# Four pairs of cross-attention and expert layer: the front of each expert layer is moved into the attention loop, the loops over sorted rows are reordered, and the third expert layer is written out without GpSimd

## The reference

```python
x = x + tanh(g_xattn[i]) * xattn_i(layernorm(x), ctx)     # i = 0..3
x = x + tanh(g_ffn[i])   * ffn_i(layernorm(x))

# xattn_0 and 3: 16 heads of 16; 3 with rotary positions and a window mask
# xattn_1: 16 heads of 64, keys and queries scaled to length 1, a null key, layernorm of the output
# xattn_2: 16 heads of 64, a given mask
# ffn_0: logits = xn @ Wr + br; softmax; the two largest of 8 experts, hidden 512, gelu, + 1 shared expert
# ffn_1: the two largest of 8, softmax over the two, hidden 1024, relu
# ffn_2: top1 = argmax(xn @ gateW.T + b)
#        out = relu(xn @ wi.T + wi_b + (xn @ A[top1].T) @ B[top1].T) @ wo.T + wo_b
# ffn_3: the two largest of softmax + bias, silu(x w1) * (x w3) @ w2, + 2 shared units
```

## Time and profile before

| | us |
|---|---|
| median of 3 runs | 2068.6 (2065.77 to 2076.95) |
| the profiled execution | 2049.69 |
| its span (first to last instruction) | 2047.9 |
| busy: PE, DVE, ACT, POOL | 1806.3, 1272.5, 974.8, 530.9 |

### The profile page before, as it was taken

How to read it: one execution, slowest core, us unless ns; L and a number is a source line. 1 busy time by engine, 2 the same in 40 slices (tenths; PEclk the granted TensorE clock), 3 DMA queues, 4 the chain that set the end, 5 groups by cost and what they waited for, 6 DMA issues and landing times. The chain is left out here.

```text
span 2047.9 us, 32584 instructions
## 1 busy us (share of the span) xinstructions
PE 1806.3 (88%) x11864; PEld 1478.7 (72%) x11864; DVE 1272.5 (62%) x2264; ACT 974.8 (48%) x1746; POOL 530.9 (26%) x465
## 2 busy tenths in 40 slices
PE   7979899977999966899999699995899799798896
PEld 4658799933677746899997378874577566588885
DVE  6877487564454545688886576666223588555654
ACT  4642367425776731577674154441233255315760
POOL 2112334263233330222222520004000045203334
PEclk9997799989999985899999799995599899789998
DMA  2004387420000003566772200001000000224753
GB/s 81 1 10 145 124 262 241 140 61 21 27 1 1 1 7 134 193 239 228 229 242 93 88 19 1 1 1 55 9 1 1 25 1 1 84 67 145 235 159 111
DMA packets 97238, 178.46 MB, mean 87 GB/s; under 512 B 24897, under 2 KB 62044, under 8 KB 96012
## 3 DMA queue, kind: packets, MB, share of 16 engines
q1 hardware_dynamic: 85594, 146.13, 21.6%
q0 software_dynamic: 11232, 30.69, 5.2%
q10 hardware_dynamic: 288, 0.00, 0.0%
HBM read 149.51 MB, written 27.26 MB: 86 GB/s over the span
## 5 line engine op out<-in xcount | busy, mean ns | idle before, releaser
L1730 POOL DMA_INDIRECT f_block_rows_home<-normed_x,f_token_of_sb x138 | 168.5, 1221 | 480.2 <-PE psum L1776 329.7
L1756 PE MATMUL psum<-f_block_h_sb,f_w1h_home 128*128 128x256 f32 x736 | 212.5, 289 | 30.2 <-DVE f_block_l_sb L1954 11.9
L1756 PE MATMUL psum<-f_block_l_sb,f_w1h_home 128*128 128x256 f32 x736 | 207.6, 282 | 0.0
L1756 PE MATMUL psum<-f_block_h_sb,f_w1l_home 128*128 128x256 f32 x736 | 207.6, 282 | 0.0
L2329 PE MATMUL psum<-a_xT_home,context_w 128*128 128x256 f32 x704 | 179.6, 400 | 14.3 <-PEq L121 13.1
L1766 PE MATMUL psum<-f_w2h_home,f_hidden_h_home 128*128 128x256 f32 x644 | 187.7, 291 | 1.9 <-DVE f_result_sb L1653 0.9
L1766 PE MATMUL psum<-f_w2h_home,f_hidden_l_home 128*128 128x256 f32 x644 | 181.9, 282 | 0.0
L1766 PE MATMUL psum<-f_w2l_home,f_hidden_h_home 128*128 128x256 f32 x644 | 181.9, 282 | 0.0
L1756 PEld LDWEIGHTS psum<-f_block_h_sb,f_w1h_home 128*128 128x128 f32 x736 | 140.8, 191 | 38.5 <-issue 28.6
L2329 PEld LDWEIGHTS psum<-a_xT_home,context_w 128*128 128x128 f32 x704 | 130.5, 195 | 45.5 <-issue 24.9
L2490 ACT ACTIVATE a_probsT_sb<-psum 77x1024 f32<-77x1024 f32 (+1 forms) x128 | 131.0, 1023 | 65.7 <-PE psum L2381 63.6
(11 more groups left out here) (327 smaller groups left out, 4066.2 us busy)
## 6 DMA issues: line engine op xcount, KB each, us to landing
f_w_sb<-in_f_w SPq DMA_DIRECT2D x161, 512.0 KB, 5.1
sorted_y<-f_result_sb SPq DMA_DIRECT2D x69, 256.0 KB, 2.2
normed_x<-f_xn_all SPq DMA_DIRECT2D x3, 2048.0 KB, 7.5
f_b_row_sb<-in_f_b SPq DMA_DIRECT2D x46, 128.0 KB, 3.5
f_w_sb<-in_f_w SPq DMA_DIRECT2D x23, 256.0 KB, 4.5
f_block_rows_home<-normed_x,f_token_of_sb POOLq DMA_INDIRECT x138, 4.3
residual<-in_x SPq DMA_DIRECT2D x8, 256.0 KB, 6.1
context_w<-in_a_wk SPq DMA_DIRECT2D x2, 1024.0 KB, 5.0
```

What stands on the lines that cost most here:

```text
L1730: nc.gpsimd.indirect_dma_start(block_rows[b % 2][:, h, :], None, xs, bass.IndirectOffsetOnAxis(ap=column, axis=0)).then_inc(sems[f"rows_in ...
L1756: last = nc.tensor.matmul(hid_ps(q)[:, m, :], w, rhs, start=(j == 0), stop=(j == len(parts) - 1))
```

## The change

1. **Front into the attention loop.** A new `front_part` is called inside `attend`. Per batch b, with its output at step s: variance on DVE at s+1 (in a1, where LAG is 3, this and all that follows 3 steps later), power on GpSimd, rows normalised on DVE at s+2, turned on PE at s+3, copied on ACT, multiplied by the router on PE at s+4, logits out on DVE at s+5. Turned rows and logits are two new uses of the spare banks. The loop is 3 steps longer (6 in a1). The rows are stored to `normed_x` batch by batch. The bias row of the shared expert (f0) and of f2 are added by GpSimd there, and the router's, shared expert's and f2's weights are loaded in the attention stage. The tables for sorting are made once in the first stage.
2. **Expert stages** begin with the choice (`Choice`, `find_rows`, `choose_low_rank`).
3. **f2** is written out: ACT rounds weights, inputs and low-rank weights, DVE makes their low parts, GpSimd has no instruction, the gate is a constant, there are no bias products.
4. **Loops over sorted blocks:** PE's order is turn of b+2, first products of b+1, second products of b; ACT takes b+2 (was b+1), DVE splits b+2 (was b+1).
5. **Context part of a1:** ten value products stand ahead of the keys' normalisation, and `take` is apart from `squares`.
6. **Combining in the tail:** f0 combines up to 1, 7, 32 of the 32 pairs behind the three blocks (was 10, 21, 32), f3 4, 12, 20, 32 (was 8, 16, 24, 32).

```diff
+def front_part(env, pair, n):
...
+    def variance(dve, b):
+        for tile in range(b * TPB, (b + 1) * TPB):
+            last = nc.vector.bn_stats(stats[:, tile, :], x[:, tile, :])
...
+        nc.vector.tensor_scalar(var[:, tiles(b)], mv[:, tiles(b), 1], EPS, None, ALU.add).then_inc(sems["var_done"], 1)
+    def power(pool, b):
+        pool.wait_ge(sems["var_done"], b + 1)
+        nc.gpsimd.tensor_tensor(rstd[:, tiles(b)], var[:, tiles(b)], half[:, tiles(b)], ALU.pow)...
+    def add_row(pool, b):
+        pool.wait_ge(sems["normed"], b + 1)
+        nc.gpsimd.tensor_tensor(x[:, tiles(b), :], x[:, tiles(b), :], row[:]..., ALU.add)...
+    def turn(pe, b, bank):
+        pe.wait_ge(sems["normed"], b + 1)
...
+    def route(pe, b, bank):
+        pe.wait_ge(sems["staged"], b + 1)
...
+    def logits_out(dve, b, bank):
+        dve.wait_ge(sems["routed"], b + 1)
...
 # attend
-    FIRST, LAST = -Q_AHEAD, GROUPS + 3
+    LAG = 3 if own else 0
+    FIRST, LAST = -Q_AHEAD, GROUPS + 6 + LAG
+        if rows_at(s) is not None:
+            uses.append(("rows", rows_at(s)))
+        if logits_at(s) is not None:
+            uses.append(("logits", logits_at(s)))
 # attend, tensor, behind output(...)
+                if rows_at(s) is not None:
+                    front["turn"](pe, rows_at(s), take_spare(pe, "rows", rows_at(s)))
+                if logits_at(s) is not None:
+                    front["route"](pe, logits_at(s), take_spare(pe, "logits", logits_at(s)))
 # attend, vector
-                if output_at(s - 1) is not None and not own:
-                    statistics(output_at(s - 1))
+                if output_at(s - 1 - LAG) is not None:
+                    front["variance"](dve, b)
+                if normed_at(s) is not None:
+                    front["normalise"](dve, normed_at(s))
+                if logits_out_at(s) is not None:
+                    front["logits_out"](dve, logits_out_at(s), spare("logits", logits_out_at(s)))
 # routed_experts, tensor
         def body(b, i, s, ahead):
             for u in range(per_expert):
+                if u == per_expert - 1 and ahead >= 2:
+                    turn(b + 2, *later(i, s, 2))
                 if u + 1 < per_expert:
                     first(b, i, s, u + 1)
                 elif ahead:
                     first(b + 1, *later(i, s, 1), 0)
-                if u == per_expert - 1 and ahead >= 2:
-                    turn(b + 2, *later(i, s, 2))
                 second(b, i, s, u)
 # routed_experts, vector
-                if u == 0 and not silu and not begins(b) and ahead >= 1:
-                    split_block(b + 1, (s + 1) % 2)
+                if u == per_expert - 1 and ahead >= 2:
+                    split_block(b + 2, s % 2)
 # context_part, a1, tensor
+        for j in range(VALUES_FIRST):
+            value_products(pe, j)
 # experts (f2), scalar and vector, in place of gpsimd
+        high(w1h[0][:], w1raw[0][:], "w1_high")
+        t["exponentials"](act)
+        high(xh[:, :, chunk(0)], xT[:, :, chunk(0)], "x_high")
...
+        weight_lows(0, 1)
+        x_low(0)
+        low(lbl[:], lb[:], lbh[:], "lora_low")
+        inputs_low(0)
...
```

1055 lines of the change are left out of this document (501 added, 554 removed).

## The result

The changed kernel takes 2054.5 us (median of 14 runs, 2044.9 to 2061.2), the kernel before 2065.5 in the same set (14 runs): a ratio of 0.9938, interval 0.9918 to 0.9959. That is 13 us faster by the ratio and 11 by the medians. In a later set it was 2026.9 against 2045.8 (0.9923, 0.9892 to 0.9953), 16 or 19 us. The forecast was 33 us (0.984): right in sign and inside its range, but almost three times what the first set shows and about twice what the later one does.

The account below looks back on a forecast made before the run. PE was taken as the bound, by its work, lower clock and waits. Terms 58 - 61.5 - 54 + 17.4 + 1.5 + 5.5 + 1 - 1 = -33 took 2068.6 to 2036 us; range 1994 to 2060.

Parts of the forecast that it names:

- Attention loops, +58 forecast: Loops a0 to a3: added turn and router products plus new waits lengthen the four loops by 58 us; lower bound 32.
- a1 (14.2 forecast): a1's loop: query products wait for the turned rows' copy on ACT, about 0.9 us a block; 14.2, bounds 8 and 25.
- rival 3: DVE and GpSimd hold each other up in the attention loops, mattering in a0 and a3: 22 us, 2058; chance 0.10.
- a2, 23.7 forecast: a2's loop: value products wait 2.9 us a block for DVE's late logits read-out; 23.7 us, bounds 8 and 45.
- Rival 4: a1 and a2: late read-outs cost PE a whole softmax step per block, 59 us more, 2095; chance 0.05.
- Fronts removed, -61.5: f0, f1, f3: only a short tail remains before the choice, saving 20.8, 19.7 and 21.0 us.
- f2, -54: a2's last output product to f2's products' end: 159 us against 212.7, first product at 25.8; bounds -60 and -42.
- f0's loop, +17.4: f0's sorted blocks: period rises from 6.73 to 7.6 us over 20 blocks, +17.4; bounds -9 and +30.
- The circle: f0's loop: turn, copies, weight splitting and result read-out run serially between second products, which need the freed bank; 7.6 us.
- Context part of a1, +15.9: Value products wait for read-outs and delay key squares: last key at 516 against 512; +5.5 net, bounds -8 and +10.
- 1 (no wait bites): Attention loops grow by PE's work alone (+32) and f0's loop gains 9: 1984 us; chance 0.20.
- 2: Larger waits: a1 and a3 at upper bounds, f0's loop +30, f2 -42; 2085 all together, two give 2060; chance 0.10.

Follow-up runs that it names:

- second profile: For the changed kernel: the same kernel run again, no edit, 2026.9 us, 0.9923. For the kernel before: run once more, no edit, 2065.7 us, 1.0019.
- the run four: Changed kernel with result read out first in f0 and f1, logits read ahead of softmax in all attention stages, a1's old context order: 1948.8 us, 0.9549.
- Result first: Changed kernel with DVE reading out block b-1's result ahead of the block's and weights' low parts in f0's and f1's loops: 2018.9 us, 0.9797.
- third set: A later set of runs on another chip: kernel before 2045.8 us, changed kernel unedited 2026.9 us, ratio 0.9923.
- the one run made for them: Changed kernel with 24 (f0) and 16 (f1, f3) of the 32 gathers left out, buffers combined as they lie: 2022.2 us, 0.9889.

## Why the prediction was wrong, point by point

**Attention loops, +58 forecast**, +79 seen, from the first to the last output products (8.4, 14.1, 42.8 and, second profile, 13.8). a0 (8.5 forecast) came as worked out. a1 (14.2 forecast) has the right size by luck. The sum had a query product wait 0.9 a block for the turned rows' copy; that wait is 0.45 and comes four times. What the sum did not have are the output products waiting 1.56 us for DVE to read out the logits, four times, 6.2 us in all:

```profile
653.80 7.15 PE L2391 MATMUL psum<-a_wo_sb,a_attT_sb 128*128 128x256 f32 x32 [1.56 <-DVE f_logits L927]
```

It is a2's circle in small, and the run four, where the early read-out takes it away, shows it. a3 took 2.2 us a block more against 1.7; 0.7 of it is DVE's normalising beside GpSimd's addition of the bias row, the hold-up of rival 3, though only there. In a0 no such thing: 385 ns.

**a2, 23.7 forecast: the step that failed.** The mechanism and the wait were right, 3.0 us for `f_low_rank` in five blocks and 1.2 in a sixth. (The read-out was put at 7.6 us behind the output product, though the parts named for it make only 6.1; it is done at 7.5, of which 1.1 is a wait of DVE for the scores.) The price was wrong. The sum took a wait for its own length; a2 grew by 42.8 us from the first to the last output product (168.8 to 211.6). 8.6 is the new work, as the run with early logits shows (177.4), 16.2 the waits, and the remaining 18 the products at 1.2 GHz behind them. The granted clock gives the same by another way: of 34 us at 0.50 half is lost, 17. The run with the logits read early removes the waits and brings back both, 34 us. Rival 4, a whole step lost, came to nearly the same length by another way: a block of 33.8 in place of 26.2 (forecast 30.2).

**Fronts removed, -61.5.** f0 -20.3, f3 -21.0, f1 -21.8. Right, but for 2 us in f1: the last output product of a1 that I read at 750.64 is the second half of one that starts at 746.64, so the front removed was 4 us longer than I took, and the choice comes 20.1 us behind the product's start against 19.1.

**f2, -54.** From a2's last output product to f2's end 154.9 us, 154.5 in the second profile (158 forecast). The first product comes at 28.4 against 25.8; behind it the products take 126.5 against 132.5, at a clock of 1.00 where the earlier trace rows had 0.97, which was not foreseen. The size is right, the parts less so.

**f0's loop, +17.4.** The circle has the period of the forecast, 7.62 against 7.6. Result first breaks it, and PE has no wait left; the old order as well, at 6.7. Right. PE's own work, taken as 6.3, is 6.1. In f1, taken at +0.5, the new order costs 5 us against the old one in the same kernel (273.3 and 278.4), which the rest of the change paid back.

**Context part of a1, +15.9 from its start** (5.5 net): +19.9 without waits for instructions. Four us off. The keys' chain was taken to be held by the values alone; DVE's later combining, which was priced at 0, holds it too. The two overlap: the order costs 6 us beside the late combining (155.3 against 149), and 24 beside the old one (158.4 against 134.2 in the runs with the old combining).

**What the sum did not have.** Waits for instructions. The profile of before, from which all its terms come, had one, of 10.5 us; its second profile had more, worth 16 us in f3's tail and 5 in f0's. They lengthen the changed kernel's first profile by 26 us and its second by none. By the medians the kernel before is 18 us shorter in the third set than in the first ones, and the changed kernel 28. f3's tail, with the wait in every profile of the first set and in none of the later ones, is 16 and 13 us of that. So these waits can account for the kernels' different times in the sets, and for the gain being smaller in the first, though only profiles, one per kernel and set, show them. Between the profiles with the fewest waits (2044.3 and 2019.0 at the last DVE row) the gain is 25 us, 8 from the forecast: a2 cost 20 and the context part 4 more than forecast, f2's products and the context part behind them 12 less, the others 4 less. The 12 are luck as far as a2 goes: they have another cause, and without them the forecast would have been 20 us off by these profiles. The sum hides a larger error than it shows. That the medians of the third set give 19 us and not 25 stays open.

**The rivals.** 1 (no wait bites) is false in a2 and f0's loop, which both cost what was said or more; the experiments make it true afterwards. 2 is false: of its four upper bounds (a1, a3, f0's loop, f2) none was reached. 3 is true in a3 and small, 0.7 us a block. 4 comes nearest in size, since a2 grew by 42.8 us where a lost step gives 45, but its mechanism is false: no step is lost, the clock falls. In a1 it is false in size too.

What stays open: what makes the waits for instructions come, and whether that is what they are. They stand behind loops, in code that runs once, in tails with gathers; they go with the set, that is with the chip or the time of the run, and the one run made for them fell in a set without them. Open too is why the clock falls behind one wait of 2.70 us and not behind the next like it.

## What to carry to other kernels

Ahead of a bound engine, a wait of a few microseconds in each turn of a loop is to be priced with the clock that follows it: look whether the products behind a wait take twice as long as those ahead of it. When work is added to a loop with an order of its own, place the instruction that frees a shared buffer by who waits for it, not at the end of the step: the two read-outs moved ahead were worth 26 and 29 us by the ratios. A term that comes out right is checked by its wait, too: a1's sum was met to 0.1 us by another wait than the one in it. And one profile is one execution on one chip: compare stage by stage with a second one, from another set, before a stage's difference is believed.

## What the runs showed of the hardware that I had not expected

- A wait of 3.0 us on PE in a loop that had been at 1.00: score products 1.12 us ahead and 1.99 behind, the clock at 0.50 for 10 us there and for 3.4 to 6.8 behind the others; mean clock 0.91 over the loop. Waits of 1.27 us in each 7.62 of f0's loop and of 1.56 in each 32.1 of a1's left it at 1.00, and one of 2.70 in a3 brought it down in five of eleven profiles.
- Waits without a releaser, of 10 to 16 us on PE, ACT or DVE, in code behind a loop that is run once, present in one set of runs and absent in another with the same kernel: 26 us between two profiles of it.
- DVE's normalising of a tile takes 0.40 us alone or beside GpSimd's copy of 0.36 us, and 1.06 when it meets GpSimd's addition of 1.27.
